# An mLSTM and expert block on one core: when the row scatters may start, and the order of a few steps at the seams

## What is computed

```python
xn = _layernorm(x)
s = attention(xn)
for i in range(E):
    h = xn @ w1[i] + b1[i]
    a, g = split(h, 2)
    y = (a * sigmoid(g)) @ w2[i] + b2[i]
    out = out + where(top1 == i, y, 0)
x = x + s * silu(out)
```

## Time and profile before

| what | value |
|---|---|
| median of 3 runs | 235.09 us (234.85 to 235.75) |
| the profiled execution: its own time | 235.47 us |
| its span, first to last instruction | 233.7 us |
| busy PE, DVE, ACT, POOL | 217.2, 162.4, 140.3, 92.6 us |
| mean granted TensorE clock | 0.985 of full speed |
| attention loop, first weighing to the last one's end | 40.1 to 102.8 us |

### The profile page before, as it was taken

One profiled execution on the slowest core, in us unless ns is written; L12 is line 12 of the kernel. 1 busy time (PEld: TensorE's weight loads), 2 busy tenths in 40 slices (PEclk: granted clock), 3 DMA queues, 4 the chain that ended last, 5 costly groups with the idle time before them and its releaser, 6 DMA issues.

```text
span 233.7 us, 6082 instructions
## 1 busy us (share of the span) xinstructions
PE 217.2 (93%) x1824; PEld 173.1 (74%) x1834; DVE 162.4 (69%) x491; ACT 140.3 (60%) x326; POOL 92.6 (40%) x130
## 2 busy tenths in 40 slices
PE   8998989678899889999999999999999999998994
PEld 6787654234545454569999999999999999996541
DVE  5998699507467658755877987798779967963170
ACT  2398758456767676877556655665566555552044
POOL 5667930756566563000333333333433333335100
PEclk9999999976999999999999999999999999999999
DMA  6999999930179111400077021011101001000498
GB/s 180 328 363 418 337 205 210 209 111 34 49 202 327 35 48 44 129 3 28 18 223 255 14 67 57 23 57 56 47 28 52 22 26 35 17 22 13 110 341 267
DMA packets 23617, 29.26 MB, mean 125 GB/s; under 512 B 3319, under 2 KB 18687, under 8 KB 23585
## 3 DMA queue, kind: packets, MB, share of 16 engines
q1 hardware_dynamic: 18994, 20.42, 26.5%
q0 software_dynamic: 3424, 8.36, 14.5%
q10 hardware_dynamic: 1168, 0.10, 0.4%
HBM read 19.99 MB, written 9.34 MB: 126 GB/s over the span
## 4 chain that ended last, share of the span: by engine, by line
PE 73%; DVE 13%; issue 5%; ACT 2%; another core or an unknown queue 2%; DMA 2%; POOL 0%; DVEq 0%; SPq 0%; ACTq 0%
PE bank L1213 15%; PE bank L1222 15%; PE head_bank L1213 15%; PE head_bank L1171 5%; PE bank L1183 4%; DVE cm L876 4%; PE bank L1161 3%; DVE stats L711 2%; PE bank L1199 2%; PE head_bank L1141 2%; PE bank L1285 2%; DMA x_sb<-in_L_attn_x 2%; PE bank L1288 1%; PE head_bank L1285 1%
## 5 line engine op out<-in xcount | busy, mean ns | idle before, releaser
L450 POOL DMA_INDIRECT y_tokens<-ffn,idx x39 | 38.6, 991 | 88.1 <-DVE ffn L1004 87.5
L876 DVE TENSOR_TENSOR cm<-dm,head_bank 128x1024 f32<-128x1024 f32 (+1 forms) x32 | 29.1, 951 | 23.7 <-PE head_bank L1171 8.5
L444 POOL DMA_INDIRECT xs_sorted<-xn,pos x32 | 31.1, 973 | 28.0 <-PE head_bank L1171 10.5
L1222 PE MATMUL bank<-w_sb,dm 128*128 x312 | 41.3, 275 | 0.1
L1213 PE MATMUL bank<-xsT,wc 128*128 128x128 f32 x320 | 39.0, 275 | 0.0
L1222 PEld LDWEIGHTS bank<-w_sb,dm 128*128 128x128 f32 x312 | 38.0, 192 | 0.3 <-issue 0.3
L1213 PEld LDWEIGHTS bank<-xsT,wc 128*128 128x128 f32 x320 | 37.3, 192 | 0.0
L1213 PE MATMUL head_bank<-xsT,wc 128*128 128x128 f32 x304 | 37.0, 275 | 0.0
L1213 PEld LDWEIGHTS head_bank<-xsT,wc 128*128 128x128 f32 x304 | 35.5, 192 | 0.0
L586 ACT ACTIVATE wc<-w_sb 128x512 f32 x39 | 24.6, 630 | 14.4 <-issue 14.3
L565 ACT ACTIVATE dm<-bank 128x512 f32<-128x512 f32 x48 | 27.0, 597 | 8.1 <-PE bank L1161 7.5
(11 more groups left out here) (192 smaller groups left out, 345.5 us busy)
## 6 DMA issues: line engine op xcount, KB each, us to landing
x_sb<-in_L_attn_x SPq DMA_DIRECT2D x16, 256.0 KB, 5.1
w_sb<-in_L_ffn_w SPq DMA_DIRECT2D x8, 512.0 KB, 8.9
w_sb<-negated_rows POOLq DMA_DIRECT2D x8, 508.0 KB
xs_sb<-xs_sorted SPq DMA_DIRECT2D x13, 192.0 KB
xs_sorted<-b_sb SPq DMA_DIRECT2D x1, 2048.0 KB, 11.1
w_sb<-y_tokens SPq DMA_DIRECT2D x8, 256.0 KB, 4.4
out_x<-w_sb SPq DMA_DIRECT2D x8, 256.0 KB, 2.5
y_tokens<-ffn,idx POOLq DMA_INDIRECT x39, 2.3
```

Source lines behind the costliest of these rows:

```text
L444: pool.indirect_dma_start(xs_dram, bass.IndirectOffsetOnAxis(ap=pos[:, t:t + 1], axis=0), xn[:, t, :], None).then_inc(s_scat, 16)
L450: pool.indirect_dma_start(y_dram, bass.IndirectOffsetOnAxis(ap=idx[:, j:j + 1], axis=0), ys_sb[:, j // CH % 2, j % CH, :], None, bounds_ch ...
L876: dve.tensor_tensor(cm[:, b % 2, :, m0:m1, :], dm[:, b % 2, :, m0:m1, :], head_bank[:, :, m0 * P:m1 * P].rearrange("p h (m t) -> p h m t", ...
L1222: last = pe.matmul(bank[6 + j % 2][:, 0:D], uT[:, j % 2, c, :], w2_sb[:, bass.ds(e * (HC * D) + c * D, D)], start=(c == 0), stop=(c == HC ...
```

## The change

Seven small edits in one:

- Every scatter waits for `s_cm` (half weighings) in place of `s_sc` (scores). `SCAT_AT[t]` becomes `2 + t * 26 // T`: scatters 0 and 1 wait for 2 half weighings, the last one for 27, which is the first half of sequence 13. That is one scatter for most half weighings and two for six of them, spread over the weighings of sequences 0 to 13.
- The last two steps of `positions()` and the third `left` row move behind the weighing of sequence 0.
- On PE and ACT, `token_rows(14)` and `outputs(14)` move behind `hidden(0)` and `gate(0)`.
- ACT's sigmoid of block 36 moves ahead of the gate of block 38.
- DVE's silu of block 36 moves ahead of the product of block 38.
- DVE's silu of block 37 moves ahead of the bias of block 38.
- The six matmuls on zeros in the tail go.

```diff
-    SCAT_AT = [t * 13 // T for t in range(T)]
+    SCAT_AT = [2 + t * 26 // T for t in range(T)]
...
             for t in range(T):
-                if SCAT_AT[t] != (SCAT_AT[t - 1] if t else 0):
-                    pool.wait_ge(s_sc, SCAT_AT[t])
+                pool.wait_ge(s_cm, SCAT_AT[t])
...
                     gate(0)
+                    outputs(b - 1)
...
-                if b + 1 < B:
+                if b + 2 < B:
                     outputs(b)
...
+                if j == NBLK - 1:
+                    sigmoid(j - 2)
                 if 1 <= j < NBLK:
                     gate(j)
...
+                if j >= 2 and j != NBLK - 1:
+                    sigmoid(j - 2)
...
                 blocks = experts_of_blocks()
-                for place in positions():
-                    link(place)
+                places = positions()
+                link(next(places))
                 dve.tensor_scalar(left[:, 1, :], sel[:, 0, :], lmask[:, 0, 1:2], lmask[:, 1, 1:2], ALU.mult, ALU.add).then_inc(s_lf1, 1)
-                left_rows(2)
                 for b in range(B):
                     weigh(b)
+                    if b == 0:
+                        for place in places:
+                            link(place)
+                        left_rows(2)
...
+                if j >= NBLK - 1:
+                    silu(j - 2)
                 if 1 <= j < NBLK:
                     product(j)
...
-                if j >= 2:
+                if 2 <= j < NBLK - 1:
                     silu(j - 2)
                     step(normals)
...
                     hidden(0)
+                    token_rows(b - 1)
...
-                if b + 1 < B:
+                if b + 2 < B:
                     token_rows(b)
...
             for g in range(NPC):
-                if g == NPC - 1:
-                    keep_warm(6, g)
                 pe.matmul(bank[g][:, :], ident[:, :], x_sb[:, g * TP:(g + 1) * TP, :], start=True, stop=False)
```

More of the change, by code:

```diff
@@ L615, in gate, with sigmoid @@
                                ACT.Sigmoid).then_inc(s_th, 1)
+            def sigmoid(j):
+                act.wait_ge(s_yb, j + 1)
+                if j >= 2:
+                    act.wait_ge(s_ye, j - 1)
+                act.activation(sy[:, j % 2, :], yb[:, j % 2, :], ACT.Sigmoid).then_inc(s_sy, 1)
             decay(0, 0)
```

## The result

The changed kernel takes 246.93 us (median of 4 runs, 245.67 to 248.1) against 235.42 in runs of the kernel before on the same chip: ratio 1.0475, 95% interval 1.040 to 1.055. It is slower, by more than the rival of the held turns gave (239.3), and outside the range. The profiled execution took 248.1 us, with a span of 246.3.

The account below looks back on a forecast made before the run. Bound taken: attention's turns, lengthened by PE signals late under scatters. Start 2.7 + turns 2.75 - loads 0.2 + seam 0.4 + silus 1.0 + zeros 0.5 = 7.15 us less than 235.09, so 228.0 us; range 222.5 to 235.

Parts of the forecast that it names:

- the rival of the held turns: Attention, sequences 2 to 13: all 11 turns held by a scatter, 4.63 us each; 239.3 us, slower; chance 0.16.
- What bounds the kernel: Turns of attention, before the experts: a signal of PE that falls into a scatter comes late; 3.85 us per turn.
- Start: Up to the weighing of sequence 2: 49.5, between 48.5 (scores done) and 50.4 (copy held too); 2.7 us less.
- Turns: Attention, sequences 2 to 13: 0.4 us of holding per turn, 3.60 us against 3.85; 2.75 us less over 11 turns.
- The sentence on POOL's time: Attention: scatters need POOL as long as 11 turns, so hardly a signal finds a gap; held against the 224.1 us rival.
- the case that everything slips through: Attention: signals 0.46 us after a scatter's start still free, turns 3.25 us, gain 6.6; 224.1 us; chance 0.15.
- The last scatter and the loads: Start of the experts: last row scatter 1.4 us after sequence 13's weighing starts, so loads may come late; 0.2 us charged.
- The seam: Attention to experts: `hidden(0)` fills PE's idle 0.50 us in front of the transposes of sequence 14; 0.4 us less.
- Silus: Tail: earlier silus of blocks 36 and 37 break up the row of scatters, last scatter sooner; 1.0 us less.
- Zeros: Tail: matmuls taking 2.75 us of PE go, but most of the saving waits for transfers; 0.5 us less.
- The clock in the tail: Tail: a granted clock of 1.00; a fall without the matmuls on zeros was excluded.
- The rival that I made of it: Scatters are not the cause: start 0.9 us, turns nothing, seam and tail 1.7 net; 232.5 us; chance 0.12.

Follow-up runs that it names:

- The memsets: Changed kernel with a fill of about 1 us on POOL in place of each row scatter, the 32 scatters behind the last: 265.16 us (one execution), 3.25 per turn.
- the best run: Changed kernel with another scatter rule: four at the start, 28 over the scores of sequences 2 to 13 in twos and threes: 230.37 us, ratio 0.977.
- those with bounds: Bounds check added to the row scatters: on the changed kernel 240.45 us; on the changed kernel with four scatters at the start 236.76 us.

## Why the prediction was wrong

*What bounds the kernel* was right: the turns of attention, and signals of PE that come late beside a scatter. The memsets show that it is the scatters, and where the scatters stand was worth 11.5 us one way and 5 us the other.

*Start* was right, and its better branch came true. Less the 1.67 us by which this execution reached the steps ahead of the positions later (the step of line 845 at 39.41, its line 840 before at 37.74), the first weighing came 0.97 us earlier (0.9 forecast) and that of sequence 2 3.7 us earlier (2.7 forecast). That is 50.20 - 1.67 = 48.53, where the text had 48.5 for scores that are done when the fourth scatter ends; it then took the middle between this and a held copy.

*Turns* is the step that failed. "So with a weighing at T the first scatter of a turn starts at T + 1.4, the second 1.27 us later at T + 2.67, a third at T + 3.94": the times were right (75.72 - 74.22 = 1.50). What I then weighed was only whether the scores end beside the second scatter, as though each turn's scatters were a row of their own. The third ends at T + 3.94 + 0.97 = 4.91, and by my own turn of 3.60 the next turn's first half is done at 3.60 + 1.22 = 4.82. The rows had to join, and nothing in the text asks what happens under a row of five. Against the 39.8 us of eleven turns of 3.62, the three long turns cost 23.1 - 3 x 3.62 = 12.2 us, and the two slow ones behind them 11.8 - 2 x 3.62 = 4.6 us. These two are rows of three under which PE, late from the hold before, ends its scores beside the third scatter; I had a third scatter at T + 3.94 and never let a signal meet it. The clock is a third thing that I left out, and a smaller one. The holds of 1.3 us in rows of three left it at 1.00, as the same stretch of the best run shows, and the long holds did not:

```profile
48.70:90.98 42.28, 36.90 (x407) 19.80 (x414) 28.08 (x48) 30.98 (x67) 25.18 (x26) 1.00 0.32 105
```

The turns that I forecast at 3.60 take 3.62 on the mean of the six others, and that is in part luck. I put the hold between two cases by the time since the scatter's start, 0.23 us (free) and 0.60 us (held). But the free one lies under the first scatter of a row (64.54) and the held one under the third (67.08). Scores that ended only 0.13 us after the start of a second scatter came 0.75 us late (77.13 to 77.88), where I had 0.07 + 0.40; they also ended earlier, at T + 2.91 and not at T + 3.13, and the two errors cancel.

*The rival of the held turns* had the right sign and the wrong price, since it took one scatter's hold, 1.3 us, as the most that a turn can lose. Its "4.63" holds for rows of three that start right behind the weighing (4.60 to 4.66 in the best run); in the changed kernel, where they start 1.5 us after it, rows of three made 5.90 and 5.92, and rows of five 7.2 to 8.0. Rows of four, in the run that has them, made 5.7 to 5.95. What I wrote against it, that PE runs ahead after a held turn and so escapes the next one, came out the other way: after a long hold PE was behind, not ahead.

*The sentence on POOL's time* ("POOL needs 28 x 1.27 = 35.6 us for the scatters of sequences 2 to 13, as long as 11 such turns") held the answer. I used it against the case that everything slips through, not to ask for the length of the rows.

*The last scatter and the loads*: 0.2 us forecast, none found. The last scatter started at 108.31, 1.49 us after the weighing of sequence 13, and the transposes of sorted rows followed the scores of sequence 15 without a wait. *The seam*: 0.4 forecast, 0.68 found (112.23 to 111.55), and 111.55 to 111.67 in all runs that have it, but for those with bounds (111.97 and 111.99) and the one with memsets, whose loads come late. *Silus*: 1.0 forecast, 0.4 found, since the last bias waits for the silu that was put ahead of it. *Zeros*: 0.5 forecast, nothing to be seen; the last loads set the pace, and in the new tail PE waits 1.10 us for their product. The clock in the tail stayed at 1.00, as forecast.

*The page's rule.* The Trainium skill, page "SBUF — State Buffer", section "Who interferes with whom", says that PE and ACT never wait on anyone for SBUF. The rival that I made of it fell, and the rule itself is not touched: no run shows a matmul that waits for SBUF. The signals behind the matmuls are late, and of those it says nothing. That the hold outlasts the last scatter by 0.8 to 1.2 us would go with the transfer and not with the instruction. The Trainium skill, page "Perfetto Trace Analysis", section "DMA Instruction — SWDGE (GPSIMD)", says that the end which a profile shows for such a transfer is that of the making of its descriptors, and not that of the moving of data. This trace agrees: the packets of the fifth scatter run from 82.37 to 82.70, behind its end at 81.79. That they are what holds the signals is not shown.

Still open: what in a scatter holds PE's signals, and why the scatters of the experts don't. Row scatters among the experts' blocks, or rows of the experts' scatters in attention, weren't tried.

## What to carry to other kernels

Where one engine's work delays the signals of another, count how long it runs without a gap and not how much of it there is per turn. A rule that frees work by progress has to be followed over two turns: if the work of one turn ends after the next turn frees more, the pieces join, the hold grows with the row, and what comes late from it can meet the next row. Here a rule by scores with at most three scatters per row, and four at the start, gave 230.4 us, where the same 32 scatters by half weighings gave 246.9.

## What was not expected of the hardware

- PE's signals waited 4.46 us under a row of five indirect transfers of POOL (4.56 under the last such row), while fills of about the same length on POOL delayed nothing that could be seen in the turns (3.25 us).
- Scores and weighted sums that ended under the first two scatters of a row mostly came up to 0.9 us late, seldom 1.0 to 1.2, and once 1.96 (in the run with the rule alone). From the third on, in rows of three and four, they were taken up 0.8 to 1.2 us after the row's end. In rows of five without bounds four of six were; the two others, under the first row of five in either kernel with the new rule, came between 0.4 us before its end and 0.4 us behind it. Transposes under the third scatter of the first row came after some 0.5 us, and under rows of eight and ten some signals came through in the middle.
- After 3.1 us of almost idle PE the granted clock was 0.50 for at least the next 5.6 us; holds of 1.3 us left it at 1.00.
- None of the scores and sums held from the third scatter on came in one of the 0.30 us pauses of rows of three to five. Longer pauses inside a row were not tried.
